# Attention block with row maxima on VectorE: the order of the last two row-maximum tiles of an octet, and of the joining step's two waits

## What is computed

```python
xn = _layernorm(x, axis=-1)
q, k, v = relu(xn @ Wq_w.T + Wq_b), relu(keys @ Wk_w.T + Wk_b), relu(values @ Wv_w.T + Wv_b)
score = einsum('bhsd,bhtd->bhst', qh, kh) / sqrt(16)        # 16 heads of 16 columns, S = T = 1024
a = einsum('bhst,bhtd->bhsd', softmax(score, axis=-1), vh)  # keys and values are shared by all batches
y = clip((xn @ sign(weights).T) * scale + bias, -100, 100)
x = x + (a reshaped + xn) + y
```

## Time and profile before

| what | before |
|---|---|
| median of 3 runs | 2887.4 us (2884.64 to 2888.26) |
| the profiled execution's own time | 2890.34 us |
| its span in the trace | 2888.5 us |
| mean granted TensorE clock | 0.979 |
| busy: TensorE matmuls | 2809.5 us, 97% |
| busy: ScalarE | 2462.0 us, 85% |
| busy: VectorE | 2336.4 us, 81% |
| busy: GpSimd | 939.0 us, 33% |
| chain that ended last | PE 74%, issue 11%, DVE 9% |

### The profile page before, as it was taken

One profiled execution on the slowest core, in us unless ns is written; L12 is line 12 of the kernel. 1 busy time (PEld: TensorE's weight loads), 2 busy tenths in 40 slices (PEclk: granted clock), 3 DMA queues, 4 the chain that ended last, 5 costly groups with the idle time before them and its releaser, 6 DMA issues.

```text
span 2888.5 us, 61156 instructions
## 1 busy us (share of the span) xinstructions
PE 2809.5 (97%) x17860; PEld 1148.5 (40%) x17860; DVE 2336.4 (81%) x4578; ACT 2462.0 (85%) x2955; POOL 939.0 (33%) x845
## 2 busy tenths in 40 slices
PE   8899999999999999999999999999999999999996
PEld 4434343433434334343443434334343433434331
DVE  6788888888888888888888888888888888888840
ACT  4788888888888888888888888888888888888896
POOL 4304333242343314333242343314333242343001
PEclk8599999999999999999999999999999999999898
DMA  7111121121211121121121211121121121221111
GB/s 140 59 37 56 64 62 35 61 65 58 64 61 51 47 69 54 65 64 33 61 68 54 64 65 49 45 69 54 65 67 30 61 68 54 65 68 36 39 55 38
DMA packets 78637, 167.75 MB, mean 58 GB/s; under 512 B 28547, under 2 KB 32646, under 8 KB 76326
## 3 DMA queue, kind: packets, MB, share of 16 engines
q1 hardware_dynamic: 78374, 164.19, 18.9%
HBM read 36.71 MB, written 17.83 MB: 19 GB/s over the span
## 4 chain that ended last, share of the span: by engine, by line
PE 74%; issue 11%; DVE 9%; POOL 1%; DVEq 1%; POOLq 0%; ACT 0%; ACTq 0%
PE value_ps L606 27%; PE ring L628 27%; PE score_ps L592 13%; DVE mx L953 7%; PE score_ps L672 1%; PE score_ps L657 1%; PE score_ps L649 1%; PE score_ps L674 1%; PE score_ps L659 1%; PE score_ps L661 1%; POOL fin L1091 1%; DVE stats L978 1%; DVE excess L929 0%; PE ring L637 0%; DVE mx L929 0%
## 5 line engine op out<-in xcount | busy, mean ns | idle before, releaser
L801 ACT ACTIVATE probs<-score_ps 128x1024 f32<-128x1024 f32 x2048 | 1991.8, 1024 | 244.7 <-PE score_ps L592 239.4
L953 DVE TENSOR_REDUCE mx<-ring 128x1 f32<-128x512 f32 x2940 | 1890.7, 684 | 220.6 <-PE ring L628 219.0
L628 PE MATMUL ring<-kstack,qstack 48*128 48x512 f32 x3430 | 1189.3, 475 | 18.8 <-DVE mx L953 12.0
L606 PE MATMUL value_ps<-probs,vones 128*32 128x512 f32 x8192 | 1095.8, 607 | 0.8 <-ACT probs L801 0.3
L628 PEld LDWEIGHTS ring<-kstack,qstack 48*128 48x128 f32 x3430 | 488.6, 184 | 1099.9 <-DVE mx L953 1057.8
L592 PE MATMUL score_ps<-qstack,kstack 51*128 51x512 f32 x4096 | 839.9, 417 | 8.7 <-ACT probs L801 5.6
L929 DVE CUSTOM_DVE_ANT_0 excess<-ring,excess 128x512 f32<-128x512 f32 x534 | 369.2, 691 | 201.2 <-PE ring L628 186.1
L592 PEld LDWEIGHTS score_ps<-qstack,kstack 51*128 51x128 f32 x4096 | 399.2, 187 | 130.0 <-ACT probs L801 66.9
L1091 POOL TENSOR_TENSOR dense<-dense,affine 128x512 f32<-128x512 f32 x128 | 164.3, 1284 | 865.7 <-ACT dense L851 864.3
L817 ACT ACTIVATE excess<-ring 128x512 f32<-128x512 f32 x490 | 292.7, 597 | 8.0 <-PE ring L628 4.8
L606 PEld LDWEIGHTS value_ps<-probs,vones 128*32 128x32 f32 x8192 | 161.6, 108 | 323.0 <-issue 280.7
(11 more groups left out here) (93 smaller groups left out, 1474.2 us busy)
## 6 DMA issues: line engine op xcount, KB each, us to landing
qstack<-parts SPq DMA_DIRECT2D x768, 64.0 KB, 2.5
fin<-taken SPq DMA_DIRECT2D x256, 128.0 KB, 2.9
xin<-x SPq DMA_DIRECT2D x16, 1024.0 KB, 4.9
base_cur<-base_new SPq DMA_DIRECT2D x16, 1024.0 KB, 5.4
fin<-recip SPq DMA_DIRECT2D x32, 512.0 KB
out<-fin SPq DMA_DIRECT2D x32, 512.0 KB, 2.6
qstack<-proj SPq DMA_DIRECT2D x256, 12.0 KB
kstack<-base_cur SPq DMA_DIRECT2D x16, 128.0 KB, 6.2
```

The lines of the kernel that those rows point to most:

```text
L606: mm = pe.matmul(value_ps[h4 * 32:(h4 + 1) * 32, :], vones[:, 2 * tp + c, hh * HALF + side * PAIRS + 2 * g + j, :, :], probs[:, q % 2 * GR ...
L628: pe.matmul(ps[:, :], qstack[nh][rows, pair, st * P:(st + 1) * P], keys, start=True, stop=True).then_inc(s_mm, 1)
L801: nc.scalar.activation(probs[:, q % 2 * GROUP + u % GROUP, :], score_ps[src][:, :], ACT.Exp, scale=EXP_SCALE).then_inc(s_probs, 1)
L953: nc.vector.tensor_reduce(most, src[:, :], AX.X, ALU.max).then_inc(s_mx, 1)
```

## The change

The tile `(1, 1, 1)` and the tile `(0, 0, 1)` change places at the end of the octet: t6 becomes the plain one, on side 1, and t7 the joining one, on side 0. The two waits of the joining tile change places too: it waits for the relu first, and for its matmul last. The counts behind which the relu of the next octet waits follow from `OCTET.index((0, 0, 1))`, and so now count one reduction more.

```diff
-        OCTET = [(1, 0, 0), (1, 1, 0), (0, 0, "difference"), (0, 1, 0), (1, 0, 1), (0, 1, 1), (0, 0, 1), (1, 1, 1)]
+        OCTET = [(1, 0, 0), (1, 1, 0), (0, 0, "difference"), (0, 1, 0), (1, 0, 1), (0, 1, 1), (1, 1, 1), (0, 0, 1)]
...
                 src = ring[at[n]]
-                dve.wait_ge(s_mm, b * 2 * TILES + hh * TILES + n + 1)
                 if joins_difference(n):
                     dve.wait_ge(s_relu, b * 2 * DIFFS + eased(hh, n))
+                    dve.wait_ge(s_mm, b * 2 * TILES + hh * TILES + n + 1)
                     join(src[:, :], excess[:, :], most)
                 else:
+                    dve.wait_ge(s_mm, b * 2 * TILES + hh * TILES + n + 1)
                     nc.vector.tensor_reduce(most, src[:, :], AX.X, ALU.max).then_inc(s_mx, 1)
```

## The result

| what | before | after |
|---|---|---|
| median of 5 runs | 2886.3 us (2884.6 to 2888.3) | 2868.8 us (2867.8 to 2871.6) |
| ratio to before | 1 | 0.9942, 95% interval 0.9929 to 0.9954 |
| span in the profiled execution | 2888.5 us | 2866.0 us |
| granted TensorE clock | 0.979 | 0.980 |

The change is faster by 0.58%, 17.5 us; by the interval, 13 to 20 us. The forecast was 2869, with a range of 2861 to 2879.

A forecast was written before the change was run, and what follows sets the result against it. Plain octets were taken as bound by a 4.91 us loop without the join, which costs only where VectorE is late. Gains summed to 18.3 us, 2890.3 to 2872.0 profiled, 2869 from the 2887.4 median; range 2861 to 2879.

The forecast's parts named there:

- The bound: Plain octet: loop of m1, t1's reduction, m4, weighing, m6 and TensorE's order, 4.91 us, without the join.
- The price of the wait: Join meeting an idle VectorE: starts 0.77 behind m6, a plain reduction 0.54 behind its matmul; preparation costs 0.23.
- the prediction's cap: Each octet gains the smaller of 0.23 and its period's excess over a plain one on VectorE's account.
- The preparation is hidden in second place: Join as second: its 0.23 of preparation runs while t6's reduction occupies VectorE for 0.60, costing nothing.
- The rival of nothing hidden: Join's preparation starts only when the reduction before it ends, 0.23 merely moves: 2887, at most 1.5 less; chance 0.07.
- The ring's rival: m6 itself is held by t3, so earlier reading of t6 only shortens work to another wait: 2884 to 2887; chance 0.03.
- The prediction's 1.00 us: Weighing to next matmul m6 on TensorE, 1505.51 to 1506.51; cited against m6 being held by t3.
- The relu's rival: ScalarE's relu of t2 held by the join, delaying m5; 0.8 of slack, 2893 at 0.05 past it; chance 0.04.
- The sum: Gain of 1.17 per batch, 16.4 us over 14, about 0.4 at the ends, 1.5 for m3's wait: 18.3 us.
- the reciprocal: Octet with the reciprocal, 6.80 against 6.40 for its like: 0.40 excess, gain 0.23.
- the octet with bn_stats and split: Octet of period 5.52, excess 0.61: gain 0.23; the next, 5.56, with VectorE behind: gain 0.
- The projecting octets: Four octets per batch: m3's 0.03 wait for t0's reduction is on the path; 60 times is 1.8, taken as 1.5.

The follow-up runs named there:

- Experiments 3 and 4: A 192-column VectorE memset behind t7 in every octet: 3 on the kernel before, 2928.0 us; 4 on the changed kernel, 2880.2 us.
- experiment 1: Kernel before with only the places of t6 and t7 exchanged, the waits left as before: 2868.9 us.
- experiment 5: Job put ahead of m3 in octets that have both: 2873.5 us on the kernel before, 2864.8 us on the changed kernel.
- 7: Changed kernel with the eight bn_stats two duos earlier: 2867.2 us; with the job also ahead of m3, 2860.3 us, and 2857.8 us at three duos.
- experiment 6: Changed kernel with the join at t5: 2957.3 us with each pair on one side, 2865.5 us with both pairs on two sides.
- experiment 2: Kernel before with only the joining tile's two waits exchanged, t6 still joining: 2874.8 us.

## Why the prediction was right, point by point

- **The bound.** Right. The loop m1, reduction of t1, m4, weighing, m6 stands in the chain after, piece by piece, and plain octets stayed at 4.90 to 4.92. Experiments 3 and 4 show the same by force: 0.15 us more on VectorE lengthened plain octets by 0.06 before and by nothing after.
- **The price of the wait.** 0.23 was read from two pairs of starts; the starts after give it back exactly (0.77 behind m6 before, 0.54 after), and octets with only bn_stats fell by 0.21 and 0.27, the second by 0.04 more than the prediction's cap. In both the gap between m1 and m3 closed (0.92 to 0.68, medians), and m4 followed m3 by 0.60 before and after, the distance of two reductions: the matmuls waited there for VectorE's own sequence, as the prediction had it.
- **The preparation is hidden in second place.** Right: the preparation started 0.10 and 0.19 behind the start of t6's reduction, in the program's order but without waiting for that reduction's end; no idle before the join in any of the rows shown, 17 us before all of them together, of which 2.9 from 200 us on (182.6 before), and no difference between the two orders of the waits (experiment 1). The rival of nothing hidden would have given 2887.
- **The ring's rival.** It would have given 2884 to 2887. The three buffers are the same, and a change of order removed the gap before the join and gained 17.5 us. The prediction's 1.00 us was read in a plain octet; from a weighing to m6 there are 1.00 us (medians) in the octets with `bn_stats` as in the plain ones, in both kernels. In octets where VectorE is late the ring does pass the lateness on to TensorE, which is how the gain comes about: with two `bn_stats` m3 came 0.92 behind m1 before and 0.68 after.
- **The relu's rival.** Nothing of it. In the plain octet after, the join ended at 1405.31 (1404.63 and 0.68), and the relu came at 1406.19 in the timeline: 0.9 of slack, as the prediction had it.
- **The sum.** 1.29 us per batch forecast (1.17 and four times 0.03), 1.33 measured; over 14 batches of the loop the trace lost 19.1. But it is made of terms that missed on both sides, and that they cancel to 2868.8 against 2869 is luck, the more so as the median of before moved from 2887.4 (three runs) to 2886.3 (five). Right within 0.03: two bn_stats (-0.48 for -0.46), the octets behind them (-0.09 for -0.08), the split alone (-0.10 for -0.11), the reciprocal (-0.23 for -0.26 with its projecting part). Wrong: the octet with bn_stats and split lost 0.11 and the one behind it 0.10, where I had 0.23 and 0. In the first the gap between m1 and m3 closed by 0.22, as forecast, but from m6 to the next m0 it grew by 0.10; in the second the gap between m0 and m1 closed by 0.10 (medians of the records). Why the 0.10 moved is open. The octet of the turned maxima gained nothing for 0.06. **The projecting octets were the term that was mis-sized**: I took the 0.03 by which m3 starts late for the whole cost, and the three without the reciprocal gained 0.11 to 0.14 each, 0.38 per batch instead of 0.09. The wait for t0 held the job behind m3 as well, by the late load of m3's weights as the rows read (experiment 5).
- **Against it**, not foreseen: the octet in which the loop over the batches turns is 5.33 in the kernel before and 5.41 after, 0.08. In single batches it takes either value: 5.40 or more in 3 of 14 batches before, in 11 after. It is mostly 5.41 in experiment 1 too, which has the exchange of places alone, and mostly about 5.33 in those that add something to it (4, 5, 7, and 6 with the join at t5 and both pairs on two sides). Whether it belongs to the change is open. Three of the six octets with other jobs are 0.01 to 0.02 longer. That I didn't follow.

The numbers that the prediction asked for in the trace: idle before t6 of about 0.22 (0.22), none before the join (none), more idle before t1 by 0.17 to 0.24 (0.23), octets with bn_stats at 4.92 (4.94 and 4.91), the reciprocal's at 6.57 (6.57). "5.52 to 5.29" between joins came out as 5.51 in one octet and 5.31 in the next, since the join stands elsewhere in it. The last number, VectorE's total idle: it fell from 552.1 to 524.0 us (span less busy time), by 28 for a span shorter by 22.5, and its busy time didn't quite stay, 2336.4 to 2342.0.

## What to carry to other kernels

Where an engine idles for a matmul as VectorE did here, put the instruction with the least preparation first behind it, and the one that needs register and semaphore instructions of its own second, so that these run while the first is busy. Here VectorE then started 0.54 behind m6 instead of 0.77. Price such a change octet by octet: the 0.45 of idle time in a plain octet was worth nothing, and the gain was where VectorE's lateness reached the loop. Adding a small instruction on purpose told slack from bound: the same memset cost 44 us on before and 11 on the changed kernel. When a matmul waits for its buffer, look at what stands behind it on TensorE too: m3's weights were loaded 0.26 behind the score unit's start where they waited for t0 and 0.02 where they didn't, and the job behind m3 started at 0.68 and at 0.56.

## What the runs showed of the hardware

- An idle VectorE started a plain reduction 0.54 behind the start of the matmul it waited for (1074.90 to 1075.44 before, 1403.49 to 1404.03 after), and the join, with a register instruction of 0.040 and a semaphore increment of 0.021 ahead of it, 0.77 behind (1506.51 to 1507.28 before). With the register instruction run earlier it was 0.68 (1061.01 to 1061.69, experiment 2), 0.09 less. As second behind a plain reduction the join started 0.60 behind it, with no idle (1404.03 to 1404.63 after).
- The join's second instruction, which reads the accumulator, lasted 0.083 (median, before) and started together with the next reduction (both at 1507.90).
- A reduction of 128 by 512 lasts 0.68 to 0.69 and the next started 0.61 behind it (median, before). The memset of 192 columns lasts 0.218; with it between the two, the next reduction started 0.81 behind (median, experiment 3), and octets with two `bn_stats` grew by 0.15 to 0.16.
- A matmul of 128 rows of contraction started 0.42 behind a 48-row one whose weights had been loaded late, and 0.32 behind one whose weights were there early (1105.05 against 1104.63 before, 1104.23 against 1103.91 after).
- Two 48-row matmuls of 512 columns on two sides of the array started within 0.01 of each other (m6 and m7 at 1506.51 before); on one side 0.34 apart behind a weighing (1502.80 and 1503.14, experiment 6). With two pairs per octet laid on one side each, the kernel took 2957.3 us, and 2865.5 with the join in the same place and both pairs on two sides: 92 us.
